# Edge accumulation of a graph network: ScalarE copies the counts over the ring, VectorE adds the weights and one column, GpSimd converts

## The reference, cut to what matters

```
out_deg = segment_sum(ones, src);  in_deg = segment_sum(ones, dst)
agg     = segment_sum(feat[src] * ci[src, None], dst)          # counts
deg     = segment_sum(w_a, dst_a)                              # weights, with self-loops
norm    = dis[src_a] * w_a * dis[dst_a]
out     = segment_sum(h[src_a] * norm[:, None], dst_a)
```

## Time and profile before

| what | value |
|---|---|
| median of 3 runs | 2397.53 us (2389.75 to 2402.13) |
| profiled execution, span from first to last instruction | 2394.0 us |
| mean granted TensorE clock, share of full | 0.764 |
| busy over the span: PE / DVE / ACT / POOL | 82% / 57% / 42% / 40% |
| first and last add of the accumulation (L797) start at | 47.1 and 566.4 us |

### The profile page before, as it was taken

One profiled execution on the slowest core, in us unless ns is written; L12 is line 12 of the kernel. 1 busy time (PEld: TensorE's weight loads), 2 busy tenths in 40 slices (PEclk: granted clock), 3 DMA queues, 4 the chain that ended last, 5 costly groups with the idle time before them and its releaser, 6 DMA issues. The chain is left out here.

```text
span 2394.0 us, 46888 instructions
## 1 busy us (share of the span) xinstructions
PE 1970.0 (82%) x14784; PEld 1716.6 (72%) x14785; DVE 1371.8 (57%) x3363; ACT 999.8 (42%) x2697; POOL 954.4 (40%) x947
## 2 busy tenths in 40 slices
PE   7888888887999999999898477777777777777775
PEld 3666666665799999998786367676767676776765
DVE  6999999997720111442324455555555555555554
ACT  5788888885320000111213334343434343434432
POOL 3122222222000000000001477777777777777775
PEclk9999999998999999999998555555555555555555
DMA  1477766768888887785562575565555555555552
GB/s 55 82 110 129 114 115 110 127 117 197 265 312 288 293 290 285 284 297 192 179 226 87 153 183 162 159 166 155 162 162 161 161 159 163 160 162 156 160 158 64
DMA packets 225379, 416.45 MB, mean 174 GB/s; under 512 B 130818, under 2 KB 150296, under 8 KB 215448
## 3 DMA queue, kind: packets, MB, share of 16 engines
q1 hardware_dynamic: 186414, 334.76, 50.1%
q0 software_dynamic: 38784, 79.48, 12.7%
HBM read 347.71 MB, written 66.43 MB: 173 GB/s over the span
## 5 line engine op out<-in xcount | busy, mean ns | idle before, releaser
L2354 POOL DMA_INDIRECT attention_windowed_vkv<-kv_dram,ttention_windowed_vsrc x808 | 781.1, 967 | 247.0 <-issue 222.5
L2445 PE MATMUL attention_windowed_vps_e<-attention_windowed_vwe,attention_windowed_vattr 97*128 97x96 f32 x1616 | 403.7, 431 | 119.9 <-DVE ttention_windowed_vscore L2520 90.7
L2459 PE MATMUL attention_windowed_vps_s<-attention_windowed_hot,attention_windowed_vmsg 128*104 128x32 f32 x1616 | 319.8, 362 | 177.4 <-DVE attention_windowed_vmsg L2524 153.4
L2445 PEld LDWEIGHTS attention_windowed_vps_e<-attention_windowed_vwe,attention_windowed_vattr 97*128 97x128 f32 x1616 | 366.5, 332 | 125.6 <-issue 125.6
L2459 PEld LDWEIGHTS attention_windowed_vps_s<-attention_windowed_hot,attention_windowed_vmsg 128*104 128x104 f32 x1616 | 297.4, 289 | 208.9 <-DVE attention_windowed_vmsg L2524 180.1
L1273 PE MATMUL graph_layers_acc<-graph_layers_w_tab,graph_layers_g 125*96 125x125 f32 x3750 | 417.8, 269 | 0.0
L678 ACT ACTIVATE add_edges_hot_lo<-add_edges_hot_lo,parts 128x128 bf16<-128x128 bf16 x1212 | 371.4, 387 | 90.1 <-DVE add_edges_hot_lo L761 90.1
L1273 PEld LDWEIGHTS graph_layers_acc<-graph_layers_w_tab,graph_layers_g 125*96 125x96 f32 x3750 | 406.6, 163 | 0.1
L729 PE MATMUL add_edges_ps_four<-add_edges_hot,add_edges_hot_lo 128*128 128x200 bf16 x2424 | 332.0, 258 | 0.0
L1103 POOL CAST graph_layers_g<-graph_layers_w_tab 125x480 bf16<-125x480 f32 x4 | 2.3, 585 | 736.0 <-ACT graph_layers_w_tab L1150 730.0
L2387 ACT ACTIVATE attention_windowed_vmsg<-ttention_windowed_vscore 128x32 f32<-128x32 f32 x202 | 46.3, 229 | 595.1 <-DVE ttention_windowed_vscore L2520 595.1
(11 more groups left out here) (244 smaller groups left out, 2458.0 us busy)
## 6 DMA issues: line engine op xcount, KB each, us to landing
graph_layers_w_tab<-w_blocks SPq DMA_DIRECT2D x75, 1562.5 KB
graph_layers_c_tab<-c_blocks SPq DMA_DIRECT2D x56, 800.0 KB
attention_windowed_vattr<-in_attr_T SPq DMA_DIRECT2D x202, 192.0 KB, 2.7
attention_windowed_vdrow<-dstf_dram SPq DMA_DIRECT2D x202, 192.0 KB, 3.2
w_blocks<-strip SPq DMA_DIRECT2D x24, 1562.5 KB, 13.9
c_blocks<-add_edges_counts SPq DMA_DIRECT2D x24, 800.0 KB, 4.8
first_table<-c_blocks SPq DMA_DIRECT2D x19, 800.0 KB, 4.3
attention_windowed_vkv<-kv_dram,ttention_windowed_vsrc POOLq DMA_INDIRECT x808
```

Source lines behind the costliest of these rows:

```text
L2354: nc.gpsimd.indirect_dma_start(out=kv[s][:, k, :], out_offset=None, in_=kv_dram, in_offset=bass.IndirectOffsetOnAxis(ap=src4[s][:, k:k + 1 ...
L2445: nc.tensor.matmul(ps_e[s % BANKS][:, k, :], attr[:, s, k * P:(k + 1) * P], wes[:], start=True, stop=True)
L2459: last = nc.tensor.matmul(ps_s[s % 2], msg[s][:, k, :], hot[s][:, k, :], start=k == 0, stop=k == Q4 - 1)
```

## The change

Of the counts, a quad's window only shares its first column with what earlier quads wrote, since the edges are sorted. So ScalarE copies columns 1 to 19 of the counts' window over the ring (`copy_counts`), and VectorE adds column 0 alone (`add_column`) and, as before, the whole window of the weights (`add`). The ring of counts no longer has to be cleared, but for its ends. GpSimd converts a finished block of counts in one instruction (`take_counts`) instead of ScalarE in five. `BY_ACT` falls from 4 to 2, so that VectorE's `middle` takes 6 of 8 columns, and `middle` moves ahead of the first `places`. TensorE waits for the column add instead of the add. `examine_edges` also checks that quads' first nodes lie at most 19 apart.

```
-        BY_ACT = G // 2
-        CONVERT_AT = (5, 7, 8, 10, 11)
+        BY_ACT = 2
...
+            def take_counts(b):
+
+                pool.wait_ge(block_done, b + 1)
+                pool.wait_ge(column_added, 2 * (4 * (b + 2) - 2))
+                if b > 0:
+                    pool.wait_ge(counts_stored, 16 * b)
+                nc.gpsimd.tensor_copy(counts[:, :, 0:LANES], strip[:, 0, :, slot(b)]).then_inc(converted, 1)
...
-                pool.wait_ge(converted, b + 1)
-                clear(b, 0, head, heads_clear)
+                take_counts(b)
+                if b % SLOTS_B == 0:
+                    pool.wait_ge(converted, b + 1)
+                    nc.gpsimd.memset(strip[:, 0, :, 0:REACH], 0.0).then_inc(ends_clear, 1)
                 pool.wait_ge(weights_stored[b % SLOTS_B], 16 * (b // SLOTS_B + 1))
-                clear(b, 1, head, heads_clear)
-                clear(b, 0, tail, tails_clear)
-                clear(b, 1, tail, tails_clear)
+                clear(b, head, heads_clear)
+                clear(b, tail, tails_clear)
...
+            def copy_counts(q):
+
+                act.wait_ge(multiplied, q + 1)
+                if reaches(q, 1):
+                    act.wait_ge(counts_copied, q)
+                window = ps_four[q % 2][:, 0, 0:NT * REACH].rearrange("p (t n) -> p t n", n=REACH)
+                nc.scalar.activation(strip[:, 0, :, bass.ds(ats.pop(q) + 1, REACH - 1)], window[:, :, 1:REACH], ACT.Copy).then_inc(counts_copied, 1)
...
-                            u = 4 * k + j // 2
-                            if u in CONVERT_AT and reaches(r, 2):
-                                convert(r, CONVERT_AT.index(u))
+                        if j % Q4 == Q4 - 1 and g > 0:
+                            copy_counts(2 * g - 2 + j // Q4)
...
-                            pe.wait_ge(added, q - 1)
+                            pe.wait_ge(column_added, q - 1)
...
-                cells = strip[:, :, :, bass.ds(at, REACH)]
+                cells = strip[:, 1, :, bass.ds(at, REACH)]
...
+            def add_column(q, at):
+
+                dve.wait_ge(counts_copied, q + 1)
+                column = strip[:, 0, :, bass.ds(at, 1)]
+                window = ps_four[q % 2][:, 0, 0:NT * REACH].rearrange("p (t n) -> p t n", n=REACH)
+                nc.vector.tensor_tensor(column, column, window[:, :, 0:1], ALU.add).then_inc(column_added, 1)
...
                     if more:
                         lanes(g + 1, s)
+                    if before:
+                        add_column(2 * g - 1, before.pop())
...
                         third(g + 1, s)
+                        middle(g + 1, s)
                         places(g + 1, s, 0)
...
                     add(2 * g, 0, at[0])
-                    if more:
-                        middle(g + 1, s)
...
+                    add_column(2 * g, at[0])
...
                     add(2 * g + 1, 1, at[1])
+                    before.append(at[1])
```

More of the change, by code:

```diff
@@ L2157, in _ @@
             dve.drain()
[L2158 to L2159 removed]
+            nc.vector.tensor_tensor(outside[:, 0:4], most[:], limit[:], ALU.is_gt).then_inc(outside_ready, 1)
+            nc.vector.tensor_scalar(outside[:, 4:5], least[:], 0.0, None, ALU.is_lt).then_inc(outside_ready, 1)
             dve.wait_ge(src_ready, 1)
```

86 lines of the change are left out of this document (51 added, 35 removed).

## The result

The changed kernel takes 2467.7 us (median of 4 runs, 2459.1 to 2482.7) beside 2397.8 us for the kernel before (4 runs, 2389.8 to 2402.1): a ratio of 1.030, 95% interval 1.025 to 1.035. It is 70 us slower, where 40 were forecast. Of all runs told of here one, of filled, was in a slower state of the chip and is left out of the medians. The profiled execution of the changed kernel has a span of 2473.9 us, before 2394.0.

A forecast was written before the change was run, and what follows sets the result against it. VectorE bounds the kernel before; after the change TensorE would, idling behind each cast. Stage +5 us, clock +34, the rest +1 sum to +40 on 2397.5: 2437 us, range 2380 to 2500.

The forecast's parts named there:

- Add, column, middle and copy: Per-instruction times on VectorE and ScalarE from start to start: add 0.58 us, column 0.12, middle 0.47, copy 0.5.
- The hold-up: In each closing group GpSimd's cast of 2.8 us blocks VectorE instructions with two SBUF inputs; TensorE idles 2.85 us.
- Hold-up less gain: Over the stage, 24 casts give back what 101 groups win at 0.5 to 0.6 us each: 24 x 0.2 = +5 us.
- the 17.5: TensorE's round in us without the cast's idle piece; eight quads at 2.19 us with nothing late.
- The clock: TensorE's granted clock falls to half behind the idle piece of most rounds, 1.4 us each: 24 x 1.4 = +34 us.
- the shorter fall: A fall of TensorE's clock lasting 3.4 us, read at the fold near 333 us of the kernel before.
- The bound of 5 us a round: Upper limit on the price of TensorE's fallen clock; lower limit 0, taken from the longer fall near 84 us.
- The cast blocks nothing: Rival: GpSimd's cast holds VectorE up by nothing or a few tenths, 55 us less, 2342 us; chance 0.19.
- The clock holds: Rival: the cast blocks VectorE but TensorE's clock stays up, +6 us, 2403 us; chance 0.23.
- The long cast: Rival: GpSimd's cast takes 4 to 5 us, total 2466 to 2490 us; chance 0.08.
- The point of 2.7 us: Idle TensorE a round, 20.2 - 17.5, below which the changed kernel is faster and above which slower.
- TensorE becomes the bound at 4.4: In ordinary groups TensorE limits at 4.4 us, perhaps 4.5, with VectorE at 4.33 and ScalarE at 4.0.

The follow-up runs named there:

- filled: The changed kernel plus eleven one-row matmuls of 500 columns of zeros into a spare bank where TensorE waits behind the cast: 2490.9 us, 1.034 of before.
- fill_real: The changed kernel plus eleven matmuls of 128 rows x 500 columns of constants where TensorE waits behind the cast: 2410.4 us, 1.006 of before.
- six_pieces: The changed kernel with GpSimd's conversion in pieces of 3 to 5 tiles, each released as VectorE goes into an add: 2375.5 us, 0.988 of before.
- pool_cast: The kernel before with one part of the change alone, GpSimd converting a block's counts in one piece instead of ScalarE: 2442.3 us, 1.020 of before.
- half_cast2: The changed kernel with GpSimd converting only 12 of a block's 25 tiles and writing zeros in the other 13: 2393.7 us, 1.000 of before.
- write_only: The changed kernel with GpSimd's conversion replaced by a memset of the same size, counts left out of the result: 2376.7 us, 0.989 of before.

## Why the prediction was right, and where it was off

The mechanism and the sign held; one term was too small, the length of the clock's falls.

- **VectorE and ScalarE.** Add, column, middle and copy cost what was worked out (670, 195, 575 and 565 ns in the mean of their groups; middle 0.47 us from start to start), and where the clock is full most quads of ordinary groups follow at 2.19 us, TensorE's own pace.
- **The hold-up.** Cast 2.87 us for 2.8, third from 1.2 to 3.9 us after the lanes' start for 4.0, TensorE idle 2.84 us for 2.85. With the clock held (fill_real) the ordinary round is 20.9, some 0.4 of it the filling, for 20.4. Hold-up less gain was +5 us in the sum and is at most 16. That the round comes out so near has some luck in it: without a cast it has 19.3 and not the 17.5 that the sum builds on, but 0.8 us of that, the wait of the register loads, runs inside the hold-up (TensorE starts 0.06 us after the column in the changed kernel, 0.8 after it in six_pieces).
- **The clock: the mis-sized term.** "I expect the shorter fall, 3.4 us, behind most of them ... 1.4 us: 24 x 1.4 = +34 us". Measured: 155 us at the lower level, 6.5 us a round, and 57 us between fill_real and the changed kernel, 2.4 a round. A fall came behind most casts, 16 of 24, as expected, but only five of them were the short one; falls of 17 us like that from 87 to 104 are in the trace beside them. The bound of 5 us a round held; the choice of the short fall did not. The reason given, a fold of the kernel before, had TensorE idle for 1.38 us; a piece twice as long was taken to end in the same fall.
- **The rivals.** "The cast blocks nothing" falls by third's 3.28 us. "The clock holds" named 2403; fill_real, where it is made to hold, has 2410. The long cast didn't come in the changed kernel; in pool_cast it did (3.96 us), by waiting and not by its size.
- **The point of 2.7 us** of idle time is wrong in both its parts: the clock's price belongs in it (half_cast2), and the gain of 55 us that it was set against doesn't exist with a whole store: 29 to 30 us in write_only and six_pieces. "TensorE becomes the bound at 4.4" left out its register loads behind the store, 1 us a round, and the folds. That row was to be had: in the kernel before the same gap is 2.97 against 2.8 elsewhere, hidden under VectorE.

What makes a fall of the clock 3 us or 20 us long, and why eight casts had none behind them, isn't settled.

## What to carry to other kernels

Before work is moved to GpSimd, look at what it reads and at what VectorE does in those microseconds: portions of 0.5 to 0.7 us, each released as VectorE goes into an instruction with a PSUM input, cost next to nothing (six_pieces, 0.988 of before), where one of 2.9 us a round cost the whole gain and 70 us more (1.030). An idle piece on TensorE is priced with the clock behind it: of the 4.1% between the changed kernel and write_only, 2.4% were the clock (57 us) and 1.7% the wait itself. And when an engine becomes the bound, look again for what its slack had hidden, its queue's register loads beside large transfers too.

## What the runs showed of the hardware

- One-row matmuls neither held the clock (0.84 with TensorE busy 434 of 450 us) nor raised it (54 in a row, 22.7 us, at 420 ns each). Matmuls over 128 rows did: constants held it (1.00), and even zeros raised it (44 in 12.15 us).
- The granted clock fell behind 16 of the 24 idle pieces of 1.9 to 3.0 us that the casts left on TensorE, for 3.4 to 24 us, though TensorE was busy again (17.7 of the 18 us from 87 to 105). The length of the idle piece didn't tell which had a fall behind them.
- A GpSimd cast that reads SBUF and a VectorE instruction with two SBUF inputs don't run together: third took 3.28 us instead of 0.68 beside a cast of 2.87. Beside a memset of 2.71 us it kept 0.68. With the same order of starts, a row of VectorE instructions went on and the cast waited (3.96 us, 16 of 24 casts of pool_cast), or the cast ran and VectorE waited.
- A GpSimd cast f32 to bf16 takes 505, 609 and 711 ns for 375, 500 and 625 elements, 1.5 us for 1500 and 2.87 us for 3125.
- TensorE stood for about 1 us in the first microseconds of a 1562 KB store out of SBUF, and the wait moved with its register loads; with the store in pieces of 312 KB the gap fell from 3.18 to 2.46 us.
